# Transformer layer in bf16: PSUM copies ahead of the residual adds at each super-tile seam, and three loads moved ahead of a stage border

## The chip, the cores and the metric

The kernel runs on the 8 cores of one Trainium2 chip; each core computes one of the 8 batch entries. The metric is the device time of the slowest core, in microseconds (us). The granted clock of TensorE is given as a share of 2.4 GHz: 1.00 is 2.4 GHz, 0.50 is 1.2 GHz.

## The reference

```python
x = L0_attn_src                                   # (8, 4096, 1024)
x = x + attn(layernorm(x), ...)
x = x + ffn(layernorm(x), weight, disha)

def attn(src, ...):                               # linear attention, 16 heads of 64
    Q, K = elu(q) + 1, elu(k) + 1
    KV = einsum('bshd,bshm->bhdm', K, v);  Z = 1 / (Q . sum(K) + EPS)
    x = layer_norm(src + (Q KV Z) @ Wo + bo, g1, be1)
    y = gelu(x @ W1 + b1) @ W2 + b2               # 1024 -> 4096 -> 1024
    return layer_norm(x + y, g2, be2)
def ffn(x, weight, disha):
    return x @ weight.T + pooled(x) @ disha
```

## The kernel before

Each core has 4096 rows of 1024 features, taken as T = 32 tiles of 128 rows. The program is a sequence of blocks (init, passA, finalize, passB1, passB2a, passB2b). At the border of two blocks every engine waits for the others. Inside a block each engine has its own instruction list, written out by hand, and runs it in order. `W(engine, key)` waits for the semaphore value that another instruction left under that key. Operations of DVE and ACT also wait for their own predecessor (helper at lines 190 to 212, so most of them carry line 207 in the profile).

passB1 ends the attention and writes x1 (after the first layer norm) to `x1_d` in DRAM, one tile at a time: POOL adds the bias (`ptt`, line 591) and ACT stores (line 772). The buffer `obf` shares its place with `x1bf`, and the second half of `srcb1` with `wfstage`.

passB2a (lines 792 to 986) is the feed-forward part. It takes the tiles in pairs, as NSUP = 16 super-tiles `st` of 256 rows. For each super-tile

- POOL loads both x1 tiles as bf16 (`xc`, line 815: `x1bf`, `x1bfB`) and, for the first NCH = 8 super-tiles, one chunk of Wf (line 826: `wfstage`); SP loads the same x1 tiles in f32 (line 802) for the residual;
- TensorE transposes the two x1 tiles into `ps_bf` and `psD` (line 846), and the chunk of Wf into `ps_bf` (line 854);
- DVE copies the transposed tiles out as `x1Ts` / `x1Ts2` (`cvxt`, key `cVxT_t`, 0.69 us each);
- TensorE goes over 32 groups c: up-projection `emit_ph(c)` (line 871, 8 matmuls of 256 columns into one of two places in `psC`), ACT applies GELU (`cAg_st_c`), down-projection `emit_py(c-1)` (line 883, four matmuls of 512 columns into `psA` and `psB`), and at the end the bias (line 898);
- DVE adds `psA` and `psB` to the f32 x1 tiles (`cvu`, key `cVu_t`, 1.23 us each), ACT squares each sum (`cSq_t`) and issues its store (line 984).

The order of work at the seam between super-tiles st-1 and st is fixed by these lists. TensorE: bias of st-1, transposes of st, Wf transposes, `emit_ph(0)`, `emit_ph(1)`, `emit_py(0)`, `emit_ph(2)`. ACT: the last GELUs of st-1, then square and store of the two sums, then (`scw`) the Wf copy, then the GELUs of st. `emit_py(0)` waits for the GELU of group 0 and, for its PSUM, for both `cvu`. `emit_ph(0)` waits for both `cvxt`. The list of DVE at the seam is

```python
                for st in range(NSUP):
                    if st >= 1:
                        cvu(2 * st - 2)
                        cvu(2 * st - 1)
                    cvxt(2 * st)
                    cvxt(2 * st + 1)
```

passB2b then does the second layer norm and the last product, and writes the output.

Of the kernel before, what the change touches and what calls it, by code (L numbers as in the profile page):

```python
# [13 lines left out]
S, D, P, T, H, DH, FF = 4096, 1024, 128, 32, 16, 64, 4096  # L14
NCH = D // P
# [20 lines left out]
def build_nc(debug=False, phases=5, marks=None):  # L36
# [9 lines left out]
    wf_d = nc.dram_tensor("Wf", [D, D], F32, kind="ExternalInput").ap()  # L46
# [23 lines left out]
    x1_d = nc.dram_tensor("x1_s", [T, P, D], F32, kind=skind).ap()  # L70
# [4 lines left out]
    with es:  # L75
# [6 lines left out]
        def VB(off, n, part=P, p0=0):  # L82
            return av[p0:p0 + part, off:off + 2 * n].bitcast(BF16)
# [14 lines left out]
        x1bfB = VB(209920, D)  # L98
# [4 lines left out]
        wfstage = VB(28672, D)  # L103
# [16 lines left out]
        x1bf = VB(32768, D)  # L120
# [55 lines left out]
        sem = {}  # L176
# [6 lines left out]
        ct = Ctr()  # L183
# [3 lines left out]
        def W(eng, key):  # L187
            if key in lookup:
                name, val = lookup[key]
                eng.wait_ge(sem[name], val)  # L190

        def I(inst, name, n=1, key=None):
            inst.then_inc(sem[name], n)
            ct.inc(name, n, key=key)

        def serial(eng, name):
            class _P:
                def __getattr__(self, attr):
                    if attr in ("wait_ge",):
                        return getattr(eng, attr)  # L200
                    fn = getattr(eng, attr)

                    def call(*a, key=None, **kw):
                        c = ct.c.get(name, 0)
                        if c > 0:
                            eng.wait_ge(sem[name], c)  # L206
                        inst = fn(*a, **kw)  # L207
                        inst.then_inc(sem[name], 1)
                        ct.inc(name, 1, key=key)
                        return inst  # L210
                    return call
            return _P()
# [14 lines left out]
        with nc.Block("init", no_gpsimd_drain=True) as blk:  # L227
            @blk.sync
            def _(sy):
                for dst, src in [(identb, idb_d), (identf, idf_d),  # L230
                                 (iplo, iplo_d), (iphi, iphi_d), (istk, istk_d),
                                 (onec, onec_d), (onesr, ones_d), (b1c, b1_d),
                                 (epszr, epsz_d),
                                 (g1r, g1_d), (be1r, be1_d)]:
                    sy.dma_start(dst[:, :], src).then_inc(sem["qw"], 16)
                    ct.inc("qw", 16)
                ct.marks["w_consts"] = ("qw", ct.c["qw"])
                for t in range(T):
                    W(sy, f"zV1_{t - 2}")
                    W(sy, f"zA1_{t - 2}")  # L240
                    sy.dma_start(xbuf[t % 2][:, :], x_d[t * P:(t + 1) * P, :]
                                 ).then_inc(sem[f"qx{t % 2}"], 16)
                    ct.inc(f"qx{t % 2}", 16, key=f"zx_{t}")
# [319 lines left out]
        with nc.Block("passB1", no_gpsimd_drain=True) as blk:  # L563
# [23 lines left out]
            @blk.gpsimd  # L587
            def _(gp):
                def ptt(u):
                    W(gp, f"bVx1v_{u}")  # L590
                    ii = gp.tensor_tensor(stf32[u % 2][:, :],  # L591
                                          stf32[u % 2][:, :], be1r[:, :],
                                          ALU.add)
                    I(ii, "po", key=f"bVx1_{u}")
                    ct.marks[f"bG1_{u}"] = ct.marks[f"bVx1_{u}"]

                for t in range(T):
                    if t >= 2:
                        ptt(t - 2)
                    if t % 3 == 0 and t // 3 < NCH:  # L600
                        w = t // 3
                        W(gp, f"bVt_{min(3 * w, T - 1)}")
                        gp.dma_start(w1_v[w][:, :],
                                     w1_d[w * P:(w + 1) * P, :]
                                     ).then_inc(sem["qg_w1"], 16)
                        ct.inc("qg_w1", 16, key=f"w_w1{w}")
                ptt(T - 2)
                ptt(T - 1)

            @blk.tensor  # L610
            def _(te):
# [180 lines left out]
        with nc.Block("passB2a", no_gpsimd_drain=True) as blk:  # L792
# [14 lines left out]
            @blk.gpsimd  # L807
            def _(gp):
                def xc(t):
                    if t >= T:  # L810
                        return
                    W(gp, f"bst1_{t}")
                    W(gp, f"cPt_{t - 2}")
                    xb = x1bf if t % 2 == 0 else x1bfB
                    gp.dma_start(xb[:, :], x1_d[t]  # L815
                                 ).then_inc(sem[f"qg_xc{t % 2}"], 16)
                    ct.inc(f"qg_xc{t % 2}", 16, key=f"cVcst_{t}")

                gp.dma_start(dshb[:, :], dsh_d).then_inc(sem["qg_dsh"], 16)
                ct.inc("qg_dsh", 16, key="w_dsh")  # L820
                xc(0)
                xc(1)
                for st in range(NSUP):
                    if st < NCH:
                        W(gp, f"cVW_{st - 1}")
                        gp.dma_start(wfstage[:, :],
                                     wf_d[st * P:(st + 1) * P, :]
                                     ).then_inc(sem["qg_wf"], 16)
                        ct.inc("qg_wf", 16, key=f"w_wf{st}")
                    xc(2 * st + 2)  # L830
                    xc(2 * st + 3)
# [72 lines left out]
            @blk.vector  # L904
            def _(v):
                v = serial(v, "dv")

                psDbf_v = psD.ap().bitcast(BF16)

                def cvxt(t):  # L910
                    if t >= T:
                        return
                    st = t // 2
                    sub = t % 2
                    pt = ps_bf[:, :] if sub == 0 else psDbf_v[:, 0:1024]
                    W(v, f"cPt_{t}")
                    W(v, f"cPh_{st - 2}_{NFCH - 1}")
                    x1tv = x1Ts if st % 2 == 0 else x1Ts2
                    v.tensor_copy(x1tv[:, :, sub * P:(sub + 1) * P],
                                  pt.rearrange("p (c s) -> p c s", c=NCH),  # L920
                                  key=f"cVxT_{t}")

                def cvw(st):
                    pass

                def cvu(t):
                    st = t // 2
                    sub = t % 2
                    psY = psA if sub == 0 else psB
                    W(v, f"cPyb_{st}_{sub}")  # L930
                    W(v, f"clx1_{t}")
                    if t < 2:
                        W(v, f"bst1_{T - 2 + t}")
                    W(v, f"cstu_{t - 2}")
                    W(v, f"cSq_{t - 2}")
                    v.scalar_tensor_tensor(stf32[t % 2][:, :], psY[:, :],
                                           1.0, ldf3[t % 3][:, :],
                                           ALU.mult, ALU.add,
                                           accum_out=usc[:, t:t + 1],
                                           key=f"cVu_{t}")  # L940

                for st in range(NSUP):
                    if st >= 1:
                        cvu(2 * st - 2)
                        cvu(2 * st - 1)
                    cvxt(2 * st)
                    cvxt(2 * st + 1)
                    cvw(st)
                cvu(T - 2)
                cvu(T - 1)  # L950
# [295 lines left out]
def build_full(debug=False, phases=5):  # L1246
    _, ct1 = build_nc(debug=debug, phases=phases)
    nc, _ = build_nc(debug=debug, phases=phases, marks=ct1.marks)
    return nc
# [47 lines left out]
```

## Time and profile before

| | us |
|---|---|
| median of the runs | 2400.61 |
| lowest run | 2398.38 |
| the profiled execution, its own time | 2410.05 |
| its span on the slowest core (core 7), on which all rows are | 2408.5 |
| spans of the 8 cores | 2380.1 to 2408.5 |
| passB2a on core 7, about | 1064 to 2088 |

All times in rows are us from the start of the span on core 7; durations called "mean ns of one" are in ns. Engines are PE (TensorE matmuls), PEld (its weight loads), DVE, ACT, POOL and SP; a q behind a name (ACTq, SPq) is the engine's sequencer issuing a DMA. A row of the timeline merges neighbouring instructions of one form; "x8" says how many.

### The profile page before, as it was taken

To read this page: it belongs to the slowest core of one execution; us is meant where nothing else is said; L and a number is where in the kernel's file an instruction comes from. 1 tells how busy PE (TensorE), PEld (TensorE's weight loads), DVE (VectorE), ACT (ScalarE), POOL (GpSimd) and SP (SyncE) were. 2 spreads that over 40 slices of the span, in tenths; PEclk is the share of its full clock that TensorE was granted. 3 is DMA by queue.
4 is the path that set the end of the run, shared out by engine and by line. 5 is a ranking of instruction groups with operands and counts; after the bars stand their busy time and mean duration, and the time that the engine had idled before them with its cause. 6 is when DMAs were issued, how large, how long until landed. Compare 5 with 4: busy or idle time off the path is not lost. (4 is left out here: it accounts for less than half of the span.)

```text
span 2408.5 us, 36344 instructions; the slowest of 8 cores (2380.1 to 2408.5 us)
## 1 busy us (share of the span) xinstructions
PE 1903.6 (79%) x12850; PEld 1114.5 (46%) x12850; DVE 681.2 (28%) x1115; ACT 694.8 (29%) x1295; POOL 233.4 (10%) x218
## 2 busy tenths in 40 slices
PE   0058888888886777749999999999999999666776
PEld 0024444444443333326666666666666666433333
DVE  2522222222222777740000000000000000167664
ACT  2532322223222222222222222222222222232332
POOL 2000000000000222220000000000000000022220
PEclk9999988989987989869999999999999999878787
DMA  9633222121212676540111111111111110144552
GB/s 188 188 94 79 56 63 71 44 62 44 71 26 63 174 206 188 171 126 17 39 48 49 49 49 49 45 44 45 44 45 44 45 44 27 62 160 172 176 191 97
DMA packets 66643, 208.18 MB, mean 86 GB/s; under 512 B 8419, under 2 KB 8548, under 8 KB 65444
## 3 DMA queue, kind: packets, MB, share of 16 engines
q1 hardware_dynamic: 33716, 111.33, 14.3%
q0 software_dynamic: 18928, 44.19, 10.7%
q10 hardware_dynamic: 13824, 50.34, 5.3%
q8 instruction: 108, 1.77, 0.3%
q14 instruction: 67, 0.55, 0.1%
HBM read 182.90 MB, written 58.72 MB: 100 GB/s over the span
## 5 line engine op out<-in xcount | busy, mean ns | idle before, releaser
L871 PE MATMUL psC<-arena 128*128 128x256 bf16 x4096 | 553.7, 281 | 28.0 <-ACT arena L207 24.5
L871 PEld LDWEIGHTS psC<-arena 128*128 128x128 bf16 x4096 | 412.0, 101 | 193.5 <-issue 34.8
L207 DVE SCALAR_TENSOR_TENSOR arena<-psA,arena 128x256 bf16<-128x256 f32 (+2 forms) x160 | 93.6, 585 | 1259.5 <-PE psA L898 887.5
L207 ACT ACTIVATE arena<-psC,arena 128x256 bf16<-128x256 f32 x512 | 242.8, 474 | 652.9 <-PE psC L871 652.8
L207 ACT ACTIVATE arena<-arena 128x1 f32<-128x1 f32 (+3 forms) x418 | 248.8, 595 | 418.8 <-DVE arena L207 369.0
L883 PE MATMUL psA<-arena 128*128 128x512 bf16 x1024 | 308.7, 383 | 0.0
L883 PE MATMUL psB<-arena 128*128 128x512 bf16 x1024 | 308.5, 383 | 0.0
L207 DVE SCALAR_TENSOR_TENSOR arena<-arena 128x1024 f32<-128x1024 f32 (+1 forms) x128 | 169.8, 1327 | 159.7 <-DMA arena<-u_s 63.4
L207 DVE TENSOR_SCALAR arena<-arena 128x1 f32<-128x1 f32 (+2 forms) x322 | 153.8, 478 | 68.5 <-DMA arena<-x 17.2
L883 PEld LDWEIGHTS psB<-arena 128*128 128x128 bf16 x1024 | 101.1, 99 | 123.7 <-issue 5.0
L519 PE MATMUL psA<-arena 128*128 128x256 bf16 x1024 | 157.4, 305 | 0.0
L207 ACT ACTIVATE arena<-psA 128x512 f32<-128x512 f32 (+1 forms) x96 | 71.0, 739 | 296.9 <-PE psA L519 121.5
L459 PE MATMUL ps_bf<-arena 128*128 128x128 bf16 x256 | 20.1, 222 | 139.5 <-DVE arena L207 139.5
L474 PE MATMUL psA<-arena 128*128 128x512 bf16 x256 | 81.5, 490 | 51.0 <-DVE arena L207 51.0
L519 PEld LDWEIGHTS psA<-arena 128*128 128x128 bf16 x1024 | 98.5, 106 | 35.8 <-issue 5.3
L883 PEld LDWEIGHTS psA<-arena 128*128 128x128 bf16 x1024 | 100.0, 99 | 19.1 <-issue 7.0
L207 POOL TENSOR_TENSOR arena<-arena 128x1024 f32<-128x1024 f32 x32 | 76.1, 2379 | 325.9 <-DMA arena<-x 325.7
L654 PE MATMUL psB<-arena 128*128 128x512 bf16 x256 | 85.0, 506 | 23.9 <-DVE arena L207 22.5
L815 POOL DMA_DIRECT2D arena<-x_s x32 | 16.9, 529 | 844.5 <-PE psD L846 834.7
L1193 PE MATMUL ps_bf<-arena 128*128 128x128 bf16 x128 | 14.6, 285 | 93.8 <-DVE arena L207 93.8
L591 POOL TENSOR_TENSOR arena<-arena 128x1024 f32<-128x1024 f32 x32 | 75.3, 2352 | 137.6 <-DVE arena L207 137.5
L207 DVE COPY arena<-ps_bf 128x512 bf16<-128x512 bf16 (+1 forms) x80 | 38.3, 478 | 165.6 <-PE ps_bf L459 145.3
(109 smaller groups left out, 1530.2 us busy)
## 6 DMA issues: line engine op xcount, KB each, us to landing
arena<-x SPq DMA_DIRECT2D x128, 512.0 KB, 4.5
x_s<-arena ACTq DMA_DIRECT2D x32, 512.0 KB, 4.0
arena<-x_s SPq DMA_DIRECT2D x32, 512.0 KB, 8.2
u_s<-arena ACTq DMA_DIRECT2D x32, 512.0 KB, 8.4
arena<-u_s SPq DMA_DIRECT2D x32, 512.0 KB, 6.6
out<-arena ACTq DMA_DIRECT2D x32, 512.0 KB, 8.2
arena<-W POOLq DMA_DIRECT2D x32, 256.0 KB, 7.1
qt_s<-arena POOLq DMA_DIRECT2D x32, 256.0 KB, 2.9
```

What stands on the lines that cost most here:

```text
L207: inst = fn(*a, **kw)
L459: ii = te.transpose(ps_bf[:, c * P:(c + 1) * P], sbp[:, c * P:(c + 1) * P], identb[:, :])
L474: te.matmul(psK(t)[:, nh * 512:(nh + 1) * 512], srcTs[:, w, sub * P:(sub + 1) * P], wk_v[:, w, nh * 512:(nh + 1) * 512], start=(w == 0), s ...
L519: ii = te.matmul(pq, wq_v[:, w, c * P:(c + 1) * P], srcTs[:, w, :], start=False, stop=(w == NCH - 1 and cc_ == 1))
L591: ii = gp.tensor_tensor(stf32[u % 2][:, :], stf32[u % 2][:, :], be1r[:, :], ALU.add)
L654: te.matmul(pat[:, nh * 512:(nh + 1) * 512], oTv[:, w * P:(w + 1) * P], wo_v[:, w, nh * 512:(nh + 1) * 512], start=(w == 0), stop=False)
L815: gp.dma_start(xb[:, :], x1_d[t]).then_inc(sem[f"qg_xc{t % 2}"], 16)
L871: ii = te.matmul(ph, w1_v[w][:, c * P:(c + 1) * P], x1t[:, w, :], start=(w == 0), stop=(w == NCH - 1))
L883: ii = te.matmul(psY[:, nh * 512:(nh + 1) * 512], hT[c % 2][:, sub * P:(sub + 1) * P], w2_v[c][:, nh * 512:(nh + 1) * 512], start=(c == 0) ...
L1193: ii = te.transpose(pn[:, c * P:(c + 1) * P], nbfP[u % 2][:, c * P:(c + 1) * P], identb[:, :])
```

## The change

Two edits. First, in passB2a the list of DVE at each seam has the two copies of the transposed tiles of st before the two residual adds of st-1. Second, the bf16 loads of the first two x1 tiles and the load of the first Wf chunk leave the list of POOL in passB2a and are issued by POOL at the end of its list in passB1, behind its last `ptt`, with waits for the first two stores of x1 and for the last readers of the buffers that they overwrite.

```diff
@@ passB1, POOL
                 ptt(T - 2)
                 ptt(T - 1)
+                W(gp, "bst1_0")
+                W(gp, f"bVtq_{T - 1}")
+                gp.dma_start(x1bf[:, :], x1_d[0]).then_inc(sem["qg_xc0"], 16)
+                ct.inc("qg_xc0", 16, key="cVcst_0")
+                W(gp, "bst1_1")
+                gp.dma_start(x1bfB[:, :], x1_d[1]).then_inc(sem["qg_xc1"], 16)
+                ct.inc("qg_xc1", 16, key="cVcst_1")
+                W(gp, f"bVt_{T - 1}")
+                gp.dma_start(wfstage[:, :], wf_d[0:P, :]
+                             ).then_inc(sem["qg_wf"], 16)
+                ct.inc("qg_wf", 16, key="w_wf0")
@@ passB2a, POOL
                 gp.dma_start(dshb[:, :], dsh_d).then_inc(sem["qg_dsh"], 16)
                 ct.inc("qg_dsh", 16, key="w_dsh")
-                xc(0)
-                xc(1)
                 for st in range(NSUP):
-                    if st < NCH:
+                    if 1 <= st < NCH:
                         W(gp, f"cVW_{st - 1}")
@@ passB2a, DVE
                 for st in range(NSUP):
+                    cvxt(2 * st)
+                    cvxt(2 * st + 1)
                     if st >= 1:
                         cvu(2 * st - 2)
                         cvu(2 * st - 1)
-                    cvxt(2 * st)
-                    cvxt(2 * st + 1)
                     cvw(st)
```

## Rows read from the trace of the kernel before

**Rows 1.** Windows of two stretches: length, busy us of each engine, PEclk, DMA share, GB/s.

```profile
1064.00:1080.00 16.00, 2.76 (x24) 2.32 (x25) 1.39 (x2) 0.00 (x0) 3.24 (x6) 0.50 1.03 282
1080.00:2088.00 1008.00, 962.38 (x6507) 635.45 (x6505) 58.28 (x91) 286.68 (x581) 18.47 (x35) 0.96 0.15 41
```

**Rows 2.** Waits of PE, 1066 to 2092: us in total, times, longest.

```profile
PE psC L871 <- ACT arena L207: 24.5, 10, 3.7
...
PE ps_bf L846 <- DMA arena<-x_s: 23.4, 1, 23.4
...
PE ps_bf L854 <- DVE arena L207: 17.2, 7, 2.5
```

**Rows 3.** Timeline of the seam into super-tile 7: start, us, engine, operation.

```profile
1517.84 0.62 PE L846 MATMUL ps_bf<-arena 128*128 128x128 bf16 x8
1517.86 1.23 DVE L207 SCALAR_TENSOR_TENSOR arena<-psA,arena 128x1024 f32<-128x1024 f32 x1 [59.54 <-PE psA L898]
...
1520.53 0.69 DVE L207 COPY arena<-ps_bf 128x1024 bf16<-128x1024 bf16 x1
...
1521.32 0.69 DVE L207 COPY arena<-psD 128x1024 bf16<-128x1024 bf16 x1
...
1522.20 0.33 ACTq L984 DMA_DIRECT2D u_s<-arena  x1
...
1522.27 3.31 PE L871 MATMUL psC<-arena 128*128 128x256 bf16 x16 [0.22 <-ACT arena L207]
1522.67 1.01 ACT L207 COPY arena<-ps_bf 128x1024 bf16<-128x1024 bf16 x1 [0.55 <-ACT arena L207]
...
1525.41 0.59 PE L883 MATMUL psA<-arena 128*128 128x512 bf16 x2
```

**Rows 4.** Timeline of DVE: first adds at seams 1 and 8 and behind super-tile 15.

```profile
1139.12 1.22 DVE L207 SCALAR_TENSOR_TENSOR arena<-psA,arena 128x1024 f32<-128x1024 f32 x1 [61.45 <-PE psA L898]
...
1580.44 1.23 DVE L207 SCALAR_TENSOR_TENSOR arena<-psA,arena 128x1024 f32<-128x1024 f32 x1 [58.43 <-PE psA L898]
...
2087.47 1.23 DVE L207 SCALAR_TENSOR_TENSOR arena<-psA,arena 128x1024 f32<-128x1024 f32 x1 [59.94 <-PE psA L898]
```

**Rows 5.** Timeline of the border between passB1 and passB2a.

```profile
1060.68 2.34 POOL L591 TENSOR_TENSOR arena<-arena 128x1024 f32<-128x1024 f32 x1 [6.86 <-DVE arena L207]
1063.86 0.33 SPq L795 DMA_DIRECT2D arena<-g2r  x1
...
1079.27 1.01 PE L854 MATMUL ps_bf<-arena 128*128 128x128 bf16 x8 [2.46 <-DMA arena<-Wf]
...
1081.72 1.01 ACT L207 COPY arena<-ps_bf 128x1024 bf16<-128x1024 bf16 x1
1082.82 0.47 ACT L207 ACTIVATE arena<-psC,arena 128x256 bf16<-128x256 f32 x1
...
1083.48 1.06 PE L883 MATMUL psA<-arena 128*128 128x512 bf16 x2
```

**Rows 6.** Timeline: first up-projection groups behind the seams into super-tiles 12 and 13.

```profile
1837.44 3.57 PE L871 MATMUL psC<-arena 128*128 128x256 bf16 x16 [3.37 <-ACT arena L207]
...
1901.14 3.31 PE L871 MATMUL psC<-arena 128*128 128x256 bf16 x16 [3.36 <-ACT arena L207]
```

**Rows 7.** Windows of PE alone: length, busy, PEclk, DMA share, GB/s.

```profile
1842.00:1843.00 1.00, 1.00 (x6) 0.69 1.02 418
...
1904.00:1905.00 1.00, 1.00 (x8) 0.97 1.03 293
```

**Rows 8.** Source lines 815 and 826: issue in ns, first and last start, landing.

```profile
L815 POOL DMA_DIRECT2D arena<-x_s x32: 527/527/562, 1064.8 to 1961.0; - x32
...
DMA to landing us min/median/max: 3.6/6.9/10.3
...
L826 POOL DMA_DIRECT2D arena<-Wf x8: 527/528/550, 1065.9 to 1460.5; - x8
...
DMA to landing us min/median/max: 4.0/7.3/13.1
```

## The prediction

> **What bounds the kernel now.** I read the windows by stage first. The stage that the second edit touches, B2a, runs from about 1080 to 2088 us: TensorE is busy 962 of 1008 us there and DVE 58 [rows 1]. So this stage is worth what TensorE loses between its dense stretches. The waits of TensorE over the stage name those losses: 23.4 us once for a load of x1 at the entrance, then 24.5 us and 17.2 us in many small waits that end at `ps_bf`/`psC` work [rows 2]. All of the small ones lie at the 15 seams between super-tiles. The timeline of one seam (into super-tile 7) shows what orders it [rows 3]. Call T0 the start of DVE's first add `cvu`, here 1517.86. DVE does add, add, copy, copy; the copies start at T0+2.67 and T0+3.46. TensorE has transposed both x1 tiles by about T0+1.1 and then waits for the copies; its first up-projection groups `emit_ph(0)`, `emit_ph(1)` start at T0+4.41. ACT squares each added tile behind its add, issues its store (second one at T0+4.34), copies the Wf chunk (T0+4.81, first seven seams only), and only then can do the first GELU. The first down-projection `emit_py(0)` starts at T0+7.55, and from there it is 1580.44 - 1525.41 = 55.03 us to the next T0.
>
> The period from T0 to T0 is my unit. It is (1580.44 - 1139.12)/7 = 63.05 us over the seven seams with a Wf chunk and (2087.47 - 1580.44)/8 = 63.38 us over the other eight [rows 4].
>
> **Edit one: DVE copies before it adds.** I walk the seam again with the durations of [rows 3].
> TensorE ends the `ps_bf` transposes at 1517.84 + 0.62, which is T0+0.60. A hop from ACT to TensorE is 1083.48 - 1082.82 - 0.47 = 0.19 us [rows 5]; I take the same for TensorE to DVE. The copies then start at T0+0.79 and, at their pitch of 0.79, T0+1.58; the add that used to start at T0 starts at T0+2.37. `emit_ph(0)` follows the second copy by 1522.27 - 1522.01 = 0.26 us: T0+1.58+0.69+0.26 = T0+2.53, 1.88 us sooner. That is what the edit gives.
>
> What it takes: everything that is queued on ACT behind the adds is 2.37 us later. ACT takes its instructions in order, and the GELU of group 0 stands behind square, store, square, store and the Wf copy. With a Wf chunk the copy starts at T0+4.81+2.37 = T0+7.18. From the start of such a copy to `emit_py(0)` the first super-tile shows 1083.48 - 1081.72 = 1.76 us (copy, GELU, hop) [rows 5]: `emit_py(0)` at T0+8.94 where it was T0+7.55. Without a chunk the GELU takes the copy's place, 0.47 us behind the store's issue: T0+4.34+2.37+0.47 = 7.18, plus 0.47 and 0.19 is T0+7.84. TensorE can do nothing meanwhile: `emit_ph(2)` and `emit_py(0)` both wait for that GELU. Before, the ACT chain ran beside the waiting and the two groups; now TensorE finishes both groups by about T0+4.3 (63 groups in 55.03 us are 0.87 us each) and waits 3.5 to 4.6 us for ACT.
>
> **The clock.** Before, TensorE stood still for 3.36 us ahead of `emit_ph(0)` at the later seams [rows 6], and restarted at a granted 0.5, the 1.2 GHz level. The low level lasted from the restart at 1837.44 until 1842.6 (the stretch 1842 to 1843 averages 0.69), and at the next seam from 1901.14 until 1904.1 (1904 to 1905 averages 0.97) [rows 6, 7]: 5.2 and 2.9 us, mean 4.05. Most of it fell on the two up-projection groups, which ACT's chain covers. After the change the last long stillness stands directly ahead of `emit_py(0)`, where nothing covers what follows. With the same 4.05 us at half speed, each seam loses 2.0 us there. Before rows bound this term from both sides: nothing if the clock stays up, 2.6 us if every restart is like the longer one. I take 2.0, since the new stillness is at least as long as the 3.36 us that was followed by the low level at both seams shown.
> The Trainium skill, page "TensorE: Matmul & The Clock Gate", section "HAM oscillation — how this bites in real kernels", speaks against this order: a short burst of matmuls followed by a wait leaves the next burst cold, so bursts belong on one side of the wait. By that rule the term is the 2.0 us above; if only the total stillness counted it would be near nothing. No run here shows the new pattern yet.
>
> Sum per seam. With a chunk: 8.94 + 55.03 + 2.0 = 65.97, +2.92 on 63.05; seven make +20.5. Without: 7.84 + 55.03 + 2.0 = 64.87, +1.49 on 63.38; eight make +12.0. Together +32.5 us. The last two adds of the stage keep their place.
>
> **Edit two: three loads move ahead of the stage border.** The border costs TensorE about 23 us. POOL's last add in B1 ends at 1060.68 + 2.34 = 1063.02, the other engines enter B2a at 1063.86 with SP's loads, POOL issues its x1 loads from 1064.8 and the first Wf load at 1065.9 [rows 5, 8]. The Wf load landed last, 13.1 us later, at 1079.0; its transposes (1079.27) release the first up-projection and ACT's copy, so this landing sets the entrance. The DMA engines were full the whole time (share 1.03) [rows 1].
> After the change the order on POOL is x1(0) at 1063.0, x1(1) at 1063.5, Wf at 1064.1, all ahead of SP's g2, be2 and x1 loads. The waits ahead of them (first stores, last square, last `bVt`) have ended long before. The border itself comes later, since POOL issues three DMAs of 0.53 us before it: about 1.2 us for SP, ACT and disha, whose results nobody needs for tens of us. If only the issue moves, Wf lands 1.8 us sooner. If it takes the shortest time of its rows, 4.0 us, it lands at 1068.1, 10.9 us sooner. Between them: x1(0) in its shortest 3.6 us lands at 1066.6, and the other two follow in the spacing of before, x1(1), issued one 0.53 later than 1064.8, at 1065.4 + 10.3 = 1075.7 to Wf at 1079.0, 3.3 us each: 1073.2. That is 6 us sooner, and I take -6, because SP's loads start behind the first of the three but run beside the other two.
> The Trainium skill, page "DMA: Bandwidth & Descriptors", section "Queues, rings and completion order", says that each DMA engine takes turns between the queues that have work, packet by packet. By it the head start counts only until SP's loads arrive, which is again the middle value.
>
> **The sum.** +32.5 - 6 = +26.5 us on the profiled execution's 2410.05 us (span 2408.5), +1.1%. The median of the runs is 2400.61, 9.4 us below that execution. So 2427 us.
>
> **Rivals.**
> *The clock stays up* (not slower). The stillness is now split in two by the short burst. If the burst keeps the clock at 2.4 GHz, the seams become 63.97 (+0.92, x7) and 62.87 (-0.51, x8), +2.4 us together, and with the entrance -3.6: 2397 us. With the far ends of the entrance it is -8.5 to +0.6. Against it: the new waits of 3.5 and 4.6 us alone are longer than the one of 3.36. It decides where the term is under 0.2 us a seam.
> *The clock stays up at half the seams*, a term of 1.0 us: +17.5 - 6 = +11.5, 2412 us. For it: the low level did not last equally long at neighbouring seams.
> *The early loads don't land early*, since the DMA engines are full: -1.8 in place of -6, +30.7, 2431 us. For it: the loads that gained least share behind SP's before.
> *The edit does what it says*: ACT's chain has slack enough and each seam gives back 1.88 us: -28 - 6 = -34, 2366 us. It needs the GELU not to stand behind the squares on ACT, against the program's order. Between this and the forecast decides whether `emit_py(0)` follows ACT or TensorE.
>
> **Chances.** Forecast 0.60, late loads 0.16, half the seams 0.11, clock up 0.08, edit as it says 0.02, more than +40 (each restart like the longer one, loads at -1.8: 15 x 0.6 = 9 on top of 30.7) 0.03. No change that a measurement of this kernel can tell is within 0.2%, 4.8 us. Slower: 0.60 + 0.16 + 0.11 + 0.03 = 0.90. The clock-up case straddles -4.8 us and is split: same 0.045, faster 0.035 + 0.02 = 0.055. The range goes from the half-seam case, 2411, to the longer restarts, 2440; outside lie about 0.15.
>
> **What would show it.** In the changed profile DVE's copies come first at each seam and the two up-projection groups start near T0+2.5 (T0 now being the end of the `psA` bias group, where the transposes begin); `emit_py(0)` starts near +8.9 and +7.8, with TensorE's wait before it released by ACT; the granted clock is 0.50 behind that start; periods near 66.0 and 64.9. The first Wf transposes start near 1073, and SP's g2 load about 1.2 us later than before. A period under 64 in the last eight would make the clock term wrong; `emit_py(0)` before T0+7.5 would make the ACT chain wrong.

## The result, and the profile after

The changed kernel takes 2431.33 us (median) where the kernel before takes 2401.1: ratio 1.0126, interval 1.0112 to 1.014. It is slower by 30 us; 2427 was forecast. Here and below a median is over all executions of a kernel, some of which ran in a slower state of the chip, while a ratio and its 95% interval compare the fast executions alone. The profiled execution took 2429.13 us, its slowest core (7 again) 2427.6. The mean span of the eight cores rose from 2393.0 to 2420.3 us, +27.3.

The waits of TensorE over the stage, in the changed kernel (us in total, times, longest), answer to [rows 2]:

```profile
PE psA L892 <- ACT arena L207: 59.8, 16, 4.9
PE ps_bf L855 <- DMA arena<-x_s: 17.6, 1, 17.6
PE psC L880 <- DVE arena L207: 14.7, 15, 1.9
PE ps_bf L863 <- DVE arena L207: 4.4, 7, 0.6
PE psD L855 <- DMA arena<-x_s: 4.2, 1, 4.2
```

Of the kernel before, one more line of that view belongs here:

```profile
PE psC L871 <- DVE arena L207: 3.4, 1, 3.4
```

The waits ahead of the up-projection and of the Wf transposes, which end with DVE's copies, fell from 24.5 + 3.4 + 17.2 to 14.7 + 4.4 us. (The view of before names ACT for the 24.5 us; by [rows 3] the second copy ends at 1522.01 and the up-projection starts at 1522.27, so it is the copy that it waited for.) A wait that was not in the list at all, of the first down-projection (`psA`, now line 892) for ACT, now holds 59.8 us. The edit gave back 26 us of waits and opened 60.

The same seam as [rows 3], into super-tile 7, in the timeline of the changed kernel:

```profile
1532.96 0.69 DVE L207 COPY arena<-ps_bf 128x1024 bf16<-128x1024 bf16 x1 [61.79 <-PE ps_bf L855]
...
1533.75 0.69 DVE L207 COPY arena<-psD 128x1024 bf16<-128x1024 bf16 x1
...
1534.55 1.23 DVE L207 SCALAR_TENSOR_TENSOR arena<-psA,arena 128x1024 f32<-128x1024 f32 x1
...
1534.70 1.91 PE L880 MATMUL psC<-arena 128*128 128x256 bf16 x16 [0.29 <-DVE arena L207]
...
1538.89 0.33 ACTq L993 DMA_DIRECT2D u_s<-arena  x1
1539.37 1.01 ACT L207 COPY arena<-ps_bf 128x1024 bf16<-128x1024 bf16 x1 [0.56 <-ACT arena L207]
1540.47 1.04 ACT L207 ACTIVATE arena<-psC,arena 128x256 bf16<-128x256 f32 x2
...
1541.20 1.01 PE L892 MATMUL psA<-arena 128*128 128x512 bf16 x2 [4.59 <-ACT arena L207]
```

T0 (the start of the transposes) is 1532.10 here. The up-projection groups start at T0+2.60, in place of T0+4.4, and take 1.91 us for 16 matmuls at the full clock (3.31 before at the half one). Then TensorE stands still for 4.59 us until ACT, behind both squares, both stores and the Wf copy, has done the first GELU; the down-projection starts at T0+9.10, in place of T0+7.6. The reader sees the trade in two rows: TensorE's first start comes 1.8 us sooner, its second 1.5 us later.

What follows the start runs at the half clock. Windows of TensorE at this seam (length, busy, PEclk, DMA share, GB/s; the first averages 0.93, so the fall lies inside the wait and not at the restart):

```profile
1536.00:1541.00 5.00, 0.60 (x6) 0.93 1.04 320
1541.00:1543.00 2.00, 1.80 (x5) 0.50 0.92 375
1543.00:1545.00 2.00, 2.00 (x11) 0.50 0.06 23
1545.00:1547.00 2.00, 2.00 (x8) 0.50 0.00 0
1547.00:1549.00 2.00, 2.00 (x16) 0.97 0.00 0
```

This is one of the longer low stretches: the seven periods with a chunk run from 65.5 to 67.0 us, and the one that starts here is 67.0.

First adds of DVE at seams 1 and 8 and behind super-tile 15, as in [rows 4]:

```profile
1137.67 1.23 DVE L207 SCALAR_TENSOR_TENSOR arena<-psA,arena 128x1024 f32<-128x1024 f32 x1
...
1601.55 1.23 DVE L207 SCALAR_TENSOR_TENSOR arena<-psA,arena 128x1024 f32<-128x1024 f32 x1
...
2115.69 1.23 DVE L207 SCALAR_TENSOR_TENSOR arena<-psA,arena 128x1024 f32<-128x1024 f32 x1 [59.71 <-PE psA L907]
```

The first two stand 2.38 and 2.45 us behind their T0 (transposes at 1135.29 and 1599.10), the last has no copies ahead of it. The period is (1599.10 - 1135.29)/7 = 66.26 us with a Wf chunk and (2115.69 - 1599.10)/8 = 64.57 without.

The border, as in [rows 5]:

```profile
1060.65 2.34 POOL L591 TENSOR_TENSOR arena<-arena 128x1024 f32<-128x1024 f32 x1 [6.68 <-DVE arena L207]
1062.93 0.57 POOL L611 DMA_DIRECT2D arena<-x_s  x1
...
1063.83 0.33 SPq L806 DMA_DIRECT2D arena<-g2r  x1
1064.01 0.55 POOL L617 DMA_DIRECT2D arena<-Wf  x1
...
1068.12 1.01 PE L855 MATMUL ps_bf<-arena 128*128 128x128 bf16 x8 [17.59 <-DMA arena<-x_s]
...
1073.38 1.01 PE L855 MATMUL psD<-arena 128*128 128x128 bf16 x8 [4.24 <-DMA arena<-x_s]
...
1076.11 1.01 PE L863 MATMUL ps_bf<-arena 128*128 128x128 bf16 x8 [1.72 <-DMA arena<-Wf]
...
1080.28 0.59 PE L892 MATMUL psA<-arena 128*128 128x512 bf16 x2 [0.19 <-ACT arena L207]
```

On this core the Wf transposes start 3.2 us sooner. x1(0) landed 5 us sooner (its transposes start at 1068.12 in place of 1073.21), but x1(1) came 5.3 us behind it.

One core is a poor witness here, because the landings scatter by about 2 us from core to core. From the start of POOL's last add in passB1 to the start of the first Wf transposes, in us, on cores 0 to 7:

| kernel | core 0 | 1 | 2 | 3 | 4 | 5 | 6 | 7 | mean |
|---|---|---|---|---|---|---|---|---|---|
| before | 19.4 | 20.9 | 20.9 | 20.7 | 20.9 | 20.0 | 18.7 | 18.6 | 20.02 |
| changed | 14.7 | 15.2 | 14.7 | 13.9 | 14.9 | 14.5 | 13.9 | 15.5 | 14.66 |

Core 7 has the shortest way of before and the longest of the changed kernel. Over the eight cores the early loads bring the Wf transposes, and the first down-projection with them, 5.4 us forward.

The same holds for the seams, where the cores scatter less: over the eight cores the mean period went from 62.98 to 66.13 us with a chunk and from 63.37 to 64.72 without, 22.1 + 10.8 = 32.9 us. 32.9 - 5.4 = 27.5 us stands against 27.3 by the mean spans.

### The profile page after: what moved, and what is told of

Same layout as the page of the kernel before. It is cut to its first block, busy times and chain, and to the rows that moved or that the text cites. A ratio compares the mean times of both kernels' runs of the same rounds, so it can differ in the third digit from the quotient of the medians.

```text
span 2427.6 us, 36346 instructions; the slowest of 8 cores (2412.8 to 2427.6 us)
## 1 busy us (share of the span) xinstructions
PE 1902.2 (78%) x12850; PEld 1107.3 (46%) x12850; DVE 681.4 (28%) x1115; ACT 694.2 (29%) x1295; POOL 233.8 (10%) x218
## 4 chain that ended last, share of the span: by engine, by line
PE 42%; DVE 13%; issue 5%; DMA 3%; ACT 3%; ACTq 1%; DVEq 1%; SPq 0%; POOL 0%; POOLq 0%
PE psC L880 18%; DVE arena L207 13%; PE psA L892 10%; PE psB L892 9%; ACT arena L207 3%; DMA arena<-u_s 2%; PE psA L1224 1%; PE psC L1224 1%; DMA arena<-Wf 0%; PE psB L665 0%; ACTq L993 0%; DMA out<-arena 0%; DVEq L206 0%; PE psA L907 0%; PE ps_bf L855 0%
## 5 line engine op out<-in xcount | busy, mean ns | idle before, releaser
L880 PE MATMUL psC<-arena 128*128 128x256 bf16 x4096 | 543.6, 278 | 14.7 <-DVE arena L207 14.7
L892 PE MATMUL psA<-arena 128*128 128x512 bf16 x1024 | 312.0, 387 | 59.8 <-ACT arena L207 59.8
L892 PE MATMUL psB<-arena 128*128 128x512 bf16 x1024 | 312.4, 387 | 0.0
L207 DVE SCALAR_TENSOR_TENSOR arena<-arena 128x1024 f32<-128x1024 f32 (+1 forms) x128 | 176.4, 1378 | 153.4 <-DMA arena<-x 63.9
L459 PE MATMUL ps_bf<-arena 128*128 128x128 bf16 x256 | 20.1, 222 | 144.4 <-DVE arena L207 144.4
L665 PE MATMUL psC<-arena 128*128 128x512 bf16 x256 | 82.9, 496 | 23.6 <-DVE arena L207 22.9
L826 POOL DMA_DIRECT2D arena<-x_s x30 | 15.9, 529 | 858.5 <-PE psD L855 852.4
L207 ACT COPY arena<-ps_bf 128x1024 bf16<-128x1024 bf16 x56 | 56.7, 1012 | 99.6 <-PE ps_bf L1202 75.5
```

The costliest lines, as they stand in the source:

```text
L459: ii = te.transpose(ps_bf[:, c * P:(c + 1) * P], sbp[:, c * P:(c + 1) * P], identb[:, :])
L665: te.matmul(pat[:, nh * 512:(nh + 1) * 512], oTv[:, w * P:(w + 1) * P], wo_v[:, w, nh * 512:(nh + 1) * 512], start=(w == 0), stop=False)
L826: gp.dma_start(xb[:, :], x1_d[t]).then_inc(sem[f"qg_xc{t % 2}"], 16)
L880: ii = te.matmul(ph, w1_v[w][:, c * P:(c + 1) * P], x1t[:, w, :], start=(w == 0), stop=(w == NCH - 1))
L892: ii = te.matmul(psY[:, nh * 512:(nh + 1) * 512], hT[c % 2][:, sub * P:(sub + 1) * P], w2_v[c][:, nh * 512:(nh + 1) * 512], start=(c == 0) ...
```

## The experiments

All ratios are to the kernel before. It was measured again with each of two sets of four kernels (2398.63 us with the first set, 2401.2 with the second), and each ratio is to the one of its own set. Timelines and periods below are of the slowest core of the profiled execution unless a core is named.

**The two edits apart.** The first kernel has only the three early loads:

```diff
 # the changed kernel, DVE list of before
                 for st in range(NSUP):
-                    cvxt(2 * st)
-                    cvxt(2 * st + 1)
                     if st >= 1:
                         cvu(2 * st - 2)
                         cvu(2 * st - 1)
+                    cvxt(2 * st)
+                    cvxt(2 * st + 1)
```

> Edit two alone: the three loads are issued at the end of POOL's list in B1, the order of DVE at the seams is that of before. Theory: the entrance is worth 3.2 us, as the changed kernel's own trace has it (first down-projection at 1080.28 for 1083.48), and nothing else moves: 2401.1 - 3 = 2398 us, ratio 0.9987. Rival: the loads are worth nothing by themselves (ratio 1.000). Second rival: in the changed kernel the entrance was worth the 6 us of the prediction and was given back elsewhere (ratio 0.9975).

Measured: 0.9979, interval 0.9967 to 0.9991, 2392.38 us against 2398.63. The early loads alone make the kernel faster: the interval, 2 to 8 us of 2400, leaves out no gain. It holds both 3.2 and 6 us, so the ratio doesn't choose between them; the traces do. From POOL's last add to the Wf transposes the eight cores of this kernel have 13.9 to 15.9 us, mean 14.63, where the kernel before has 20.02: 5.4 us, as in the changed kernel. The 3.2 us of the expectation were those of core 7 alone.

The second has only the new order of DVE (the diff reversed, on the kernel before):

> Edit one alone: copies ahead of adds at the 15 seams, loads as before. Theory: it carries the whole loss, 7 x 3.1 + 8 x 1.3 = 32 to 33 us by the changed kernel's periods of 66.2 and 64.7: 2434 us, ratio 1.014, first down-projection at T0+9.1 (with a Wf chunk) and T0+8.1 (without). Rival: part of the loss comes from the early loads (the tiles being loaded at other times, a later border), then this is below 1.012.

Measured: 1.014, interval 1.0122 to 1.0158, 2432.14 us against 2398.63, +33.5. The first down-projection is at T0+9.1 and T0+8.1. So the new order carries all of the loss. What the early loads take off it can't be read here, since this interval and that of the changed kernel (1.0112 to 1.014) overlap.

**ACT's order.** If the squares in front of the first GELU are what the new order runs into, taking them out of its way must turn the loss into a gain. In ACT's list of the changed kernel (`sq(t)` and `stu(t)` are the square and the store of tile t, as two functions):

```diff
                 for st in range(NSUP):
                     scw(st)
                     for c in range(NFCH):
                         ...
                         sc.activation(hT[c % 2][:, :], ph, AF.Gelu, ...)
-                    for sub in range(2):
-                        t = 2 * st + sub
-                        (square and store of t)
+                        if st >= 1:
+                            if c == 2:
+                                sq(2 * st - 2)
+                            elif c == 3:
+                                stu(2 * st - 2)
+                            elif c == 4:
+                                sq(2 * st - 1)
+                            elif c == 5:
+                                stu(2 * st - 1)
+                for t in (T - 2, T - 1):
+                    sq(t)
+                    stu(t)
```

> The changed kernel with ACT's list altered: the squares and stores of the two sums of super-tile st-1 are issued behind the GELUs of groups 2 to 5 of super-tile st, no longer ahead of the Wf copy and the first GELU. Theory (ACT's order is what the copies-first order runs into): the first GELU follows its up-projection group, the first down-projection starts near T0+4.5 and is complete when the psB add is done near T0+5.1, TensorE has no stillness above 1 us, the clock stays at 1.00 over the seams, the period falls to 59.8 in all 15: -6.2 x 7 - 4.9 x 8 = -83 us on the changed kernel, 2348 us, ratio to before 0.978. Rival A (the adds on DVE hold the down-projection just as long): first down-projection at T0+8, ratio 1.01 as before. Rival B (ACT has no room for the squares among the GELUs: 1.26 us idle per group for 1.15 us): each square delays a GELU by some tenths, up to 10 us of the gain is lost, 2358 us.

Measured: 0.978, interval 0.9763 to 0.9798, 2347.03 us against 2398.63. One seam in its timeline (core 4, T0 = 1431.13):

```profile
1433.59 1.01 ACT L207 COPY arena<-ps_bf 128x1024 bf16<-128x1024 bf16 x1 [4.52 <-PE ps_bf L863]
1433.73 1.91 PE L880 MATMUL psC<-arena 128*128 128x256 bf16 x16 [0.29 <-DVE arena L207]
...
1434.97 0.47 ACT L207 ACTIVATE arena<-psC,arena 128x256 bf16<-128x256 f32 x1 [0.38 <-PE psC L880]
...
1435.70 0.59 PE L892 MATMUL psA<-arena 128*128 128x512 bf16 x2
...
1438.54 1.06 ACT L207 ACTIVATE arena<-arena 128x1024 bf16<-128x1024 f32 x1
```

The Wf copy now waits for its transposes and not for ACT's own work, the down-projection starts at T0+4.57 directly behind the two groups, and the square stands later (1438.54), among the GELUs. The windows of this seam stay at the full clock:

```profile
1432.00:1434.00 2.00, 1.07 (x15) 1.00 0.23 27
1434.00:1436.00 2.00, 1.94 (x18) 1.00 1.12 165
1436.00:1438.00 2.00, 1.99 (x14) 1.00 1.06 310
```

13 of the 15 periods are 59.68 to 59.75 us and the last is 60.1; one (61.03, into super-tile 9) had a half-clock up-projection. At the seams without a chunk TensorE still waits 1.5 us ahead of the up-projection, where the expectation had no stillness above 1 us. The squares among the GELUs cost nothing that shows.

The same move on the kernel before, with the adds still first on DVE:

> The kernel before, with only ACT's list altered as in the run before this one (adds still first on DVE). Theory: here TensorE and not ACT ended the seam: the up-projection starts at T0+4.43 behind 3.4 us of stillness, runs at clock 0.50, and ends at T0+7.8. So moving the squares is worth next to nothing: ratio 0.998 to 1.002. Rival (ACT's queue was the bound before too): the first down-projection comes at T0+6.2, -1.5 x 15 = -22 us, ratio 0.991.

Measured: 1.0007, interval 0.9991 to 1.0023. TensorE is what ends the seam here, in the timeline (core 7, T0 = 1514.58):

```profile
1518.94 1.01 ACT L207 COPY arena<-ps_bf 128x1024 bf16<-128x1024 bf16 x1 [6.43 <-PE ps_bf L854]
1519.01 3.31 PE L871 MATMUL psC<-arena 128*128 128x256 bf16 x16 [0.21 <-DVE arena L207]
1521.08 0.47 ACT L207 ACTIVATE arena<-psC,arena 128x256 bf16<-128x256 f32 x1 [1.12 <-PE psC L871]
...
1522.16 0.59 PE L883 MATMUL psA<-arena 128*128 128x512 bf16 x2
```

ACT is 6.43 us idle ahead of its copy and the down-projection still starts at T0+7.58, behind 3.31 us of half-clock matmuls. So neither move gains anything alone (+33.5 and 0 us); both together, with the early loads, are worth 52 us. The early loads are about 5 of them; both moves without the loads were not run.

**The clock, by itself.** To take the stillness away without touching ACT:

```diff
                         emit_ph(c)
+                        if c == 1 and st >= 1:
+                            for _k in range(20 if st < NCH else 16):
+                                te.matmul(psD[:, 0:512], identb[:, :],
+                                          w2_v[0][:, 0:512],
+                                          start=True, stop=True)
```

> The changed kernel with matmuls of 512 columns put on TensorE between the second up-projection group and the first down-projection of super-tiles 1 to 15 (20 where a Wf chunk is copied, 16 where not); they write psD, which nobody reads then, and the result doesn't use them. They do no useful work: they only keep TensorE active for 4.3 and 3.5 us while it waits for ACT. Theory (the clock term is real): the clock stays at 1.00 over the seam, the first down-projection stays at T0+9.1 and T0+8.1, the periods fall to 64.1 and 63.1, together 2.0 x 7 + 1.65 x 8 = 27 us off the changed kernel: 2404 us, ratio to before 1.001. Rival (the down-projections behind the wait are slow for another reason, or the fillers only add work): ratio 1.013 or more.

Measured: 1.0028, interval 1.0013 to 1.0042, 2408.44 us against 2401.2; 23 us off the changed kernel, of 27 expected. The seam into super-tile 6 (core 5), start of the fillers and of the down-projection, and the windows:

```profile
1460.17 4.48 PE L903 MATMUL psD<-arena 128*128 128x512 bf16 x20
...
1464.97 0.59 PE L892 MATMUL psA<-arena 128*128 128x512 bf16 x2 [0.33 <-ACT arena L207]
```

```profile
1458.00:1461.00 3.00, 2.71 (x23) 1.00 0.91 103
1461.00:1465.00 4.00, 3.67 (x18) 1.00 0.97 224
1465.00:1468.00 3.00, 3.00 (x20) 1.00 1.00 408
```

The down-projection starts as late as without fillers (T0+9.15) and then runs at full clock: matmuls that do nothing take about 2.1 us off a period with a chunk (64.16 for 66.26). At two of the last eight seams the clock had already fallen under the up-projection; there the fillers themselves ran slowly and pushed the down-projection to T0+9.5 for T0+8.1, which is 2.8 of the missing 4 us.

**Half of the ACT chain.** Only the second square and its store go behind the GELUs. ACT's list, against the one with both moved:

```diff
-                            if c == 2:
-                                sq(2 * st - 2)
-                            elif c == 3:
-                                stu(2 * st - 2)
-                            elif c == 4:
+                            if c == 4:
                                 sq(2 * st - 1)
                             elif c == 5:
                                 stu(2 * st - 1)
+                    (behind the last group: sq(2 * st), stu(2 * st))
```

> The changed kernel with only the second square and its store behind the GELUs; the first stays ahead of them. Half of the ACT chain (1.74 us) is gone. Theory: the first down-projection starts at T0+7.35 (with a chunk) and T0+6.3, TensorE stands still for 2.8 and 1.8 us ahead of it. If the clock still falls there as before (2.0 and 1.7 us), the periods are 64.4 and 63.0 and the ratio 1.001; if a stillness of this length no longer lowers it, 62.4 and 61.3, ratio 0.990. Rival (ACT's chain isn't what holds the down-projection): 1.012.

Measured: 0.9924, interval 0.99 to 0.9948, 2383.55 us. The down-projection starts at T0+7.40 and T0+6.35, as laid out. The clock did neither of the two things laid out at all seams. On core 1 the periods with a chunk are 65.6, then 62.4 to 62.6 (nothing lost) and 64.1 (1.7 lost) in turn. Those without are 61.36 to 61.64 (nothing lost) up to the last, of 62.8. But nothing lost isn't the clock staying up at each of them. Two neighbouring seams, into super-tiles 8 and 9 (T0 = 1576.32 and 1637.68):

```profile
1578.92 1.91 PE L880 MATMUL psC<-arena 128*128 128x256 bf16 x16 [1.53 <-DVE arena L207]
1582.67 0.59 PE L892 MATMUL psA<-arena 128*128 128x512 bf16 x2 [1.84 <-ACT arena L207]
```

```profile
1640.28 3.28 PE L880 MATMUL psC<-arena 128*128 128x256 bf16 x16 [1.54 <-DVE arena L207]
1644.03 0.59 PE L892 MATMUL psA<-arena 128*128 128x512 bf16 x2 [0.47 <-ACT arena L207]
```

At the second the low level lay over the up-projection (3.28 us for the 16 matmuls), as it did at five of the eight seams without a chunk on this core. That shortened TensorE's wait for ACT and moved nothing: the down-projection starts at T0+6.35 at both. So a low stretch is paid for where it falls. Beside ACT's chain it is free, behind it it costs.

**SP held back at the border.** One line ahead of SP's g2 load in passB2a, `W(sy, "w_wf0")`:

> The changed kernel with SP waiting for the landing of the first Wf chunk before it issues its g2, be2 and x1 loads in B2a. Theory (the early loads gained 3.2 and not 6 us because SP's loads run beside them): x1(1) and Wf land in the spacing of a free queue, about 1.6 us each, Wf at about 1070 in place of 1075.9, 5 us sooner: ratio 0.998 of the changed kernel, 1.0105 to before. Rival (the early loads are slow by themselves, by their conversion to bf16 or the store before them): less than 1 us, ratio 1.0125.

Measured: 1.0099, interval 1.0079 to 1.0119, 2425.6 us. The interval overlaps that of the changed kernel, so the timeline (core 5) is the better witness:

```profile
1051.59 2.34 POOL L591 TENSOR_TENSOR arena<-arena 128x1024 f32<-128x1024 f32 x1 [6.70 <-DVE arena L207]
...
1060.04 1.01 PE L856 MATMUL ps_bf<-arena 128*128 128x128 bf16 x8 [20.91 <-DMA arena<-x_s]
```

```profile
1061.30 1.01 PE L856 MATMUL psD<-arena 128*128 128x128 bf16 x8 [0.24 <-DMA arena<-x_s]
...
1063.17 1.01 PE L864 MATMUL ps_bf<-arena 128*128 128x128 bf16 x8 [0.86 <-DVE arena L207]
```

From POOL's last add to the Wf transposes it is 11.58 us on this core, and 11.2 to 11.6 (mean 11.4) over the eight, where the changed kernel has a mean of 14.7 and the kernel before 20.0: 3.3 us sooner than the changed kernel, of 5 expected. x1(1) now follows x1(0) closely (TensorE waits 0.24 us for it; 4.24 on core 7 of the changed kernel), and the Wf transposes wait for a copy and no longer for the load. x1(0) itself came no sooner: its transposes start 7.7 us behind the start of POOL's last add with SP held (mean of the cores) and 7.8 without.

Both moves together:

> Squares and stores behind the GELUs of groups 2 to 5 (as in the run that gave 0.978), and SP held until the first Wf chunk has landed. Theory: the two gains add: 2347 - 5 = 2342 us, ratio 0.976. Rival (SP's x1 tiles now come too late somewhere, or the entrance gains nothing): 0.978 or more.

Measured: 0.9753, interval 0.9731 to 0.9775, 2344.84 us against 2401.2: 56 us below the kernel before by the medians, 59 by the ratio, the fastest kernel of this study. Against 0.978 without the hold the intervals overlap; that the hold adds here is likely and not shown.

## Why the prediction was right, point by point

**The ACT chain.** Forecast: add at T0+2.37, up-projection at T0+2.53, down-projection at T0+8.94 and T0+7.84. Measured: 2.45, 2.60, 9.1 and 8.06. The walk was 0.1 to 0.2 us short at each end: the first copy starts at T0+0.86 and not 0.79. That this chain holds the down-projection is shown by the runs with the squares moved (T0+4.57) and with one moved (T0+7.40).

**The clock term.** Forecast 2.0 us at every seam. From the periods, behind the measured start and 55.03 us: 66.26 - 9.1 - 55.03 = 2.1 with a chunk, 64.57 - 8.06 - 55.03 = 1.5 without. The fillers show it by removal. The mechanism was right, but the term is no constant: with a chunk single seams lost 1.3 to 1.7 us (four) and 2.7 to 2.9 (three), which is above the 2.6 that the prediction gave as its upper bound. It had the low level last from the restart; the window of 0.93 above shows that it begins inside the wait. At one seam (into super-tile 8) it lay over the up-projection:

```profile
1601.70 3.57 PE L880 MATMUL psC<-arena 128*128 128x256 bf16 x16 [1.53 <-DVE arena L207]
...
1607.16 0.59 PE L892 MATMUL psA<-arena 128*128 128x512 bf16 x2 [1.89 <-ACT arena L207]
```

The clock was back before the down-projection and the period was 63.06: the rival in which nothing is lost, at 1 of 15 seams.

**The sum of edit one.** 7 x (66.26 - 63.05) + 8 x (64.57 - 63.38) = 22.5 + 9.5 = 32.0 us on core 7, 32.9 over the eight cores; forecast 32.5 (its two addends are 20.4 and 11.9, so 32.4), and alone on the chip +33.5. That it came out to the half microsecond is luck in part: the chain was 0.16 x 7 + 0.22 x 8 = 2.9 us longer than forecast, the clock term 0.1 x 7 - 0.5 x 8 = 3.3 us smaller in sum.

**The early loads.** Forecast -6, measured -5.4 over the eight cores and -3.2 on core 7, from whose rows the forecast was made. The size is right and the way to it was not. On core 7 Wf landed at about 1075.9 and not 1073.2. x1(0) took 5 us from its issue and not its shortest 3.6, and the next two came 5.3 and 2.7 us behind it, not 3.3 and 3.3 (in the kernel before the first of these steps was 2.6, 1073.21 to 1075.79, which the prediction passed over). Against that, core 7 before was 1.4 us quicker to its Wf transposes than the mean core, so there was more to gain than its rows showed. On the mean core the new way is 1.9 us longer than forecast (2.7 on core 7, less the 0.8 by which that core is slower) and the old one 1.4 us longer. That the two nearly cancel is luck. The run with SP held shows what the second and third load ran beside. Why x1(0) takes 5 us is open, since holding SP did not shorten it. The Trainium skill, page "DMA: Bandwidth & Descriptors", section "Queues, rings and completion order", has the queues take turns packet by packet; the trace agrees, in that loads issued first and alone for a moment still ran shared with loads issued after them (14.7 us with, 11.4 us without).

**The whole.** +32.9 - 5.4 = +27.5 us is within a microsecond of the forecast +26.5, and the mean spans rose by 27.3. The median of the slowest core rose by 30 us. The rival with late loads named 2431 us, the very median, but its term of -1.8 is not what any trace of early loads shows.

**The border.** I had it 1.2 us later behind POOL's three DMA issues. It was not: SP's g2 load starts at 1063.83, before 1063.86 [rows 5], while POOL's own issues run on to 1064.5. On all eight cores it starts 3.18 to 3.22 us behind the start of POOL's last add, in both kernels. So other engines entered passB2a while POOL still worked on the DMA issues of passB1, and what is said of the kernel before, that at a border every engine waits for the others, doesn't hold for these issues. The 1.2 us step was wrong, and cost nothing in the sum since I had costed it at nothing.

**The rivals.** *The edit does what it says* fell: that needs the squares out of the first GELU's way, and with them gone the same order gave 59.75 us periods. *Late loads* fell too: -5.4 us is near the -6 and not the -1.8. *Half the seams* is what the seams with a chunk show in the kernel with one square moved, not this one.

**The Trainium skill's** page "TensorE: Matmul & The Clock Gate", section "HAM oscillation — how this bites in real kernels", says that a short burst of matmuls followed by a wait leaves the next burst cold. The trace agrees for the waits of 3.6 and 4.6 us (0.50 behind the start in the windows above). In the kernel with one square moved it held for waits of about 2.9 us at four of seven seams (core 1), and behind waits of about 1.8 us the down-projection lost nothing.

What stays open: at which seams the clock falls early. Seams of one kernel that are alike to 0.1 us in TensorE's work have the low stretch at different places, as the two above do; no run here sets it.

## What to carry to other kernels

Before moving work on one engine, write down for every engine what is queued behind the thing that gets later. Here DVE's adds looked like the laggard in front of TensorE, but they fed ACT's in-order list, in which the GELU that TensorE needs next stood behind two squares that nobody needs for 50 us. Move the work that nobody waits for first: with it moved, the kernel that had lost 30 us was 52 us faster than the one before.
A stillness of TensorE can cost twice if nothing covers what follows it (here 3.6 to 4.6 us of waiting, and behind it 1.3 to 2.9 us lost at the half clock, at all seams of core 7 but one): ask not only how long it is, but which matmuls run at half clock and who hides them.
Read a difference of a few microseconds at a single event on all cores. Here the slowest core said 3.2 us and the eight together 5.4.

## What the runs showed of the hardware that was not expected

DMA issues on POOL at the end of one block did not delay the other engines' entry into the next (1063.83 against 1063.86 us on core 7, 3.18 to 3.22 us behind the start of POOL's last add on all). Matmuls without use, put into a wait of TensorE of 3.5 to 4.6 us, made the kernel 23 us faster than the same kernel without them (2408.44 against 2431.33; 1.0028 against 1.0126 as ratios to the kernel before).
